# A latent-attention loop taken in groups of five heads, with the fifth head's latents in idle rows of the other four heads' products

## The reference, cut to what matters

```python
def _L1_ffn_ref(x, gamma_norm, Wq_w, ...):
    G, H, DQK, DV, L, D_IN = (8, 16, 128, 128, 100, 128)
    xn = _l2norm(x, d) * gamma_norm
    q = (xn @ Wq_w + Wq_b).reshape(b, s, G, H, DQK)
    ...
    qk = jnp.einsum('bsghd,blgd->bghsl', q, kc) * (1.0 / DQK ** 0.5)
    att = jax.nn.softmax(qk, axis=-1)
    z = jnp.einsum('bghsl,blgd->bsghd', att, vc).reshape(b, s, G * H * DV)
    zn = _l2norm(z, G * H * DV) * wz_g1
    h1 = jax.nn.silu(zn @ wz_w1 + wz_b1)
    h1n = _l2norm(h1, 2 * FF) * wz_g2
    return jax.nn.silu(h1n @ wz_w2 + wz_b2)
```

## Time and profile before

| | us |
|---|---|
| median of 3 runs | 3220.47 (3220.12 to 3221.82) |
| the profiled execution | 3195.91 |
| its span, first to last instruction | 3194.1 |
| TensorE matmul busy | 2906.5 (91%) |
| weight loads busy | 2407.5 (75%) |
| VectorE busy | 2374.4 (74%) |
| GpSimd busy | 2111.3 (66%) |
| ScalarE busy | 1660.1 (52%) |

### The profile page before, as it was taken

How to read it: one execution, slowest core, us unless ns; L and a number is a source line. 1 busy time by engine, 2 the same in 40 slices (tenths; PEclk the granted TensorE clock), 3 DMA queues, 4 the chain that set the end, 5 groups by cost and what they waited for, 6 DMA issues and landing times.

```text
span 3194.1 us, 46016 instructions
## 1 busy us (share of the span) xinstructions
PE 2906.5 (91%) x15508; PEld 2407.5 (75%) x15540; DVE 2374.4 (74%) x4469; ACT 1660.1 (52%) x3083; POOL 2111.3 (66%) x1634
## 2 busy tenths in 40 slices
PE   3478886778999999699999999999999999999997
PEld 2256665677888888578888888888777788888886
DVE  2589887436666666578888888888888888888886
ACT  0389885335556555245545455454444455454553
POOL 5689885005777777257777777777666677777774
PEclk9789998799999999789999999999999999999998
DMA  1111000000000000100000000000000001000000
GB/s 45 36 32 26 22 23 31 1 27 1 1 1 1 1 1 1 56 30 30 31 30 30 31 26 25 30 30 31 31 21 30 21 31 37 31 30 30 31 21 7
DMA packets 37145, 75.96 MB, mean 24 GB/s; under 512 B 10060, under 2 KB 14164, under 8 KB 36280
## 3 DMA queue, kind: packets, MB, share of 16 engines
q1 hardware_dynamic: 35384, 69.97, 6.8%
q0 software_dynamic: 1536, 3.15, 0.4%
HBM read 63.65 MB, written 1.05 MB: 20 GB/s over the span
## 4 chain that ended last, share of the span: by engine, by line
PE 53%; DVE 3%; issue 1%; POOL 0%; ACT 0%; POOLq 0%; DVEq 0%
PE lat_ps_h L1994 21%; PE lat_ps_z L2003 11%; PE lat_ps_s L1951 8%; PE lat_ps_t L1977 7%; PE lat_ps_s L1966 3%; PE lat_ps_s L1958 2%; DVE latm_newton L1737 0%; DVE latm_top L1690 0%; DVE latm_sc L1694 0%; DVE latm_attT L1708 0%; PE lat_ps_s L2023 0%; DVE latm_newton L1738 0%; DVE latm_tot L1701 0%; DVE latm_share L1725 0%; POOL lat_zz L1654 0%
## 5 line engine op out<-in xcount | busy, mean ns | idle before, releaser
L1994 PE MATMUL lat_ps_h<-latm_attT,latm_share 100*128 100x512 f32 x3072 | 831.5, 406 | 6.7 <-DVE latm_attT L1708 6.3
L1641 POOL TENSOR_TENSOR latm_att<-latm_sc,latm_tot 128x400 f32<-128x400 f32 x512 | 437.7, 855 | 532.2 <-DVE latm_tot L1703 528.4
L1860 ACT CAST latm_attT<-lat_ps_t 100x512 fp32r<-100x512 f32 x512 | 300.4, 587 | 757.3 <-PE lat_ps_t L1977 757.3
L1654 POOL TENSOR_TENSOR lat_zz<-lat_zz,lat_zsq 128x512 f32<-128x512 f32 x508 | 658.0, 1295 | 4.7 <-ACT lat_zsq L1867 4.4
L1994 PEld LDWEIGHTS lat_ps_h<-latm_attT,latm_share 100*128 100x128 f32 x3072 | 574.3, 189 | 112.4 <-DVE latm_attT L1708 9.9
L1708 DVE TENSOR_TENSOR latm_attT<-lat_ps_t,latm_attT 100x512 fp32r<-100x512 f32 x512 | 351.6, 687 | 248.3 <-ACT latm_attT L1860 247.9
L2003 PE MATMUL lat_ps_z<-latm_attT,lat_vc 100*128 100x512 f32 x1536 | 484.2, 423 | 0.0
L946 POOL TENSOR_SCALAR mha_probs<-mha_probs,mha_inv 128x1024 f32<-128x1024 f32 x128 | 364.6, 2849 | 121.6 <-DVE mha_inv L1167 121.5
L1951 PE MATMUL lat_ps_s<-latm_wk,lat_xr 128*128 128x400 f32 x1536 | 369.0, 349 | 7.7 <-DVE latm_share L1725 5.9
L452 POOL TENSOR_TENSOR ret_probs<-ret_probs,ret_shared 128x1024 f32<-128x1024 f32 x128 | 306.0, 2422 | 49.4 <-ACT ret_probs L585 49.4
L1951 PEld LDWEIGHTS lat_ps_s<-latm_wk,lat_xr 128*128 128x128 f32 x1536 | 289.0, 190 | 59.1 <-DVE latm_share L1725 11.9
(11 more groups left out here) (356 smaller groups left out, 4718.9 us busy)
## 6 DMA issues: line engine op xcount, KB each, us to landing
lat_w_in<-in_w_quads SPq DMA_DIRECT2D x64, 512.0 KB, 3.6
lat_wq_in<-in_wq_quads SPq DMA_DIRECT2D x64, 256.0 KB, 2.7
ret_qk_head<-ret_qk_parts SPq DMA_DIRECT2D x256, 32.0 KB, 2.0
moe_w<-in_W SPq DMA_DIRECT2D x2, 1024.0 KB
ret_shared<-in_xpos_q SPq DMA_DIRECT2D x1, 1024.0 KB, 5.1
ret_shared<-in_xpos_k SPq DMA_DIRECT2D x1, 1024.0 KB, 5.0
latw_wkv<-in_Wkv SPq DMA_DIRECT2D x1, 1024.0 KB
out<-latm_res SPq DMA_DIRECT2D x4, 256.0 KB, 3.3
```

Source lines behind the costliest of these rows:

```text
L1641: nc.gpsimd.tensor_tensor(att[:, k % SLOTS].rearrange("p (j l) -> p j l", j=QH), sc[:, u].rearrange("p (j l) -> p j l", j=QH), tot[:, u].u ...
L1654: nc.gpsimd.tensor_tensor(dst, dst, zsq[:, n % 2], ALU.add).then_inc(s["zz_added"], 1)
L1860: e.copy(attT[:, n % 2, 0], ps_t[0:L, :]).then_inc(s["attT_high"], 1)
L1994: mm = e.matmul(ps_h[:, f, half, :], share[:, q % 2, w_part, cols], attT[:, n % 2, a_part], start=(n % NS in (0, 4) and (a_part, w_part) = ...
```

## The change

The group becomes five heads (QH = 5): per batch 25 groups of five and one of three, 52 in all. A group of five is ten steps: j = 0 to 4 in half 0 and again in half 1. Steps stay 512.

- A tile of scores is 128 tokens against 5 x 100 latents, 500 columns; 416 tiles. They are taken at j = 0, 1, 2 (tiles 1 to 3 of the next half) and j = 3 (tile 0 of the half after it); none at j = 4.
- A product's weight has 100 of 128 rows. Now it has 125: rows 100 to 124 of head j (0 to 3) hold latents 25j to 25j + 24 of the fifth head's share, and the transposed attention carries the fifth head's weights for them in the same rows. So `add` returns at once for j = 4. The head sum and the square are still done for each head.
- To bring them there: ScalarE's new `copy_last` scales the fifth head's 100 weights of a tile by its reciprocal and writes them as quarters behind the 100 of the other four in `att` (row pitch 125); `turn`, `high` and `low` of j = 0 to 3 are 125 wide. SyncE's new `move_rows` copies four quarters of the fifth head's share from SBUF to SBUF, across partitions, once per group; for it the fifth head's piece is made first, of three pieces (heads 3 and 4; 0 and 1; 2) at j = 4 of half 0 and j = 0, 1 of half 1. `make_wk` is at j = 4 of half 1.
- `turn` of a half's first head waits for the copies of its four tiles as well; `reduce_heads` waits for `attT_ready` itself, as `add` did for it before.
- `sc` and `tot` have three buffers, LEAD is 7, and the weights of a group are loaded as five heads. The stages of batch 0's end are spaced to the longer groups.

```diff
-QH = 4
-NQ = G * GH // QH
+QH = 5
+NQ = -(-G * GH // QH)
+PART = L // (QH - 1)
+ROWS = L + PART
...
+            FIVES = B * NQ
+            heads_of = lambda q: min(QH, G * GH - q % NQ * QH)
+            full = lambda q: heads_of(q) == QH
+            group = lambda q, j: q // NQ * G + (q % NQ * QH + j) // GH
+            runs = lambda q: [(j, max(i for i in range(heads_of(q)) if group(q, i) == group(q, j)) + 1) for j in range(heads_of(q))
+                              if j == 0 or group(q, j) != group(q, j - 1)]
+            pieces = lambda q: [(3, 5), (0, 2), (2, 3)] if full(q) else [(0, 2), (2, 3)]
+
+            steps = [(q, c, j) for q in range(FIVES) for c in range(2) for j in range(heads_of(q))]
+            first_step = lambda q, c: steps.index((q, c, 0))
+            begins = [first_step(q, 0) for q in range(FIVES)] + [K]
+            adds = lambda n: sum(1 for q, c, j in steps[:n] if j < QH - 1)
+            KT = FIVES * TB
+            tile_of = lambda k: (k // TB, k % TB // 4, k % 4)
+            scored_at = []
+            for k in range(KT):
+                q, c, i = tile_of(k)
+                behind = q > 0 and not full(q - 1 if c == 0 else q)
+                scored_at.append(first_step(q, c) - ((5, 5, 4, 3) if behind else (7, 5, 4, 3))[i])
+            scored = lambda n: [k for k in range(KT) if scored_at[k] == n]
+            last_scored = lambda n: max(k for k in range(KT) if scored_at[k] <= n)
+            finished = lambda n: [k - 1 for k in scored(n) if k > 0] + [KT - 1] * (n == scored_at[KT - 1] + 1)
...
+                def move_rows(q):
+
+                    u = q % 2
+                    e.wait_ge(s["share_ready"], START + pieces_before(q) + 1)
+                    for j in range(QH - 1):
+                        e.dma_start(share[L:ROWS, u, :, j * FF2:(j + 1) * FF2].bitcast(F32),
+                                    share[j * PART:(j + 1) * PART, u, :, (QH - 1) * FF2:QH * FF2].bitcast(F32)
+                                    ).then_inc(rows_in[u], 16)
...
+                load(1)
+                for q in range(FIVES):
+                    if full(q):
+                        move_rows(q)
+                    if q + 2 < FIVES:
+                        load(q + 2)
...
+                def copy_last(k):
+
+                    if not full(k // TB):
+                        return
+                    e.wait_ge(s["inv_ready"], START + k + 1)
+                    if k >= SLOTS:
+                        e.wait_ge(s["turned"], START + first_step(*tile_of(k - 4)[:2]))
+                    e.activation(att[:, k % SLOTS].rearrange("p (j l) -> p j l", j=QH)[:, 0:QH - 1, L:ROWS],
+                                 sc[:, k % 3, (QH - 1) * L:HL].rearrange("p (j l) -> p j l", j=QH - 1),
+                                 ACT.Copy, scale=tot[:, k % 3, QH - 1:QH]).then_inc(s["copied"], 1)
...
                 def high(n):
 
+                    w = width(n)
                     e.wait_ge(s["turned"], START + n + 1)
                     if n >= 2:
                         e.wait_ge(s["z_ready"], START + n - 1)
-                    e.copy(attT[:, n % 2, 0], ps_t[0:L, :]).then_inc(s["attT_high"], 1)
+                    e.copy(attT[0:w, n % 2, 0], ps_t[0:w, :]).then_inc(s["attT_high"], 1)
...
                 def turn(n):
 
-                    half, j = n % TB // 4, n % 4
+                    q, c, j = steps[n]
+                    w, k = width(n), q * TB + 4 * c
                     if j == 0:
-                        e.wait_ge(s["weighted"], START + n + 4)
+                        e.wait_ge(s["weighted"], START + k + 4)
+                        e.wait_ge(s["copied"], START + copied_by(k + 4))
                     e.wait_ge(s["attT_ready"], START + n)
...
                 def add(n):
 
-                    q, half, j = quad(n), n % TB // 4, n % 4
-                    if n % TB == 0:
-                        e.wait_ge(s["share_ready"], START + 2 * q + 2)
...
+                    (q, c, j), w = steps[n], width(n)
+                    if full(q) and j == QH - 1:
+                        return
+                    if (c, j) == (0, 0):
+                        e.wait_ge(s["share_ready"], START + pieces_before(q + 1))
+                        if full(q):
+                            e.wait_ge(rows_in[q % 2], 16 * (QH - 1) * sum(1 for i in range(q + 1) if full(i) and i % 2 == q % 2))
...
-                                mm = e.matmul(ps_h[:, f, half, :], share[:, q % 2, w_part, cols], attT[:, n % 2, a_part],
...
+                                mm = e.matmul(ps_h[:, f, c, :], share[0:w, q % 2, w_part, cols], attT[0:w, n % 2, a_part],
...
                 def reduce_heads(n):
 
+                    q, c, j = steps[n]
                     e.wait_ge(s["squared"], START + n)
+                    e.wait_ge(s["attT_ready"], START + n + 1)
```

261 lines of the change are left out of this document (143 added, 118 removed).

## The result

The changed kernel takes 3178.7 us (median of 4 runs, 3174.8 to 3180.95) beside 3221.1 us of before: ratio 0.9865, interval 0.9848 to 0.9882. It is faster by 42 us (38 to 49 by the interval). The forecast was 112 us less; 3178.7 lies outside the range that I gave. The way was right, the size was wrong by 70 us.

The account below looks back on a forecast made before the run. TensorE was taken to bound the loop, VectorE having a fifth to spare. Products -133, scores -38, turns +19 and waits +40 sum to -112 us, off the runs' median 3220.5: 3109 us, range 3085 to 3135.

Parts of the forecast that it names:

- products dropped: TensorE in the loop: six products go in 100 of 512 steps, -133 us; extra weight rows cost nothing.
- scores: TensorE's score matmuls: 512 tiles at 0.60 us become 400 of 500 columns at 0.65 and 16 of 300, -38 us.
- wider turns: TensorE's turn loads of 125 columns for 100: 12 ns more for each of 1600, +19 us.
- waits of before that go: TensorE's ordinary waits at the spare bank's fills, 64 groups at 0.5 us, credited to the change.
- new waits, short groups: TensorE's waits in the new loop: 50 groups at 1.4 us, plus 2 us for the short groups.
- The hole: j4 steps without scores or products: the next turn waits 0.7 us after a share, 0.35 after a wk.
- VectorE: VectorE's work, 2.80 us per plain step against TensorE's 3.17, was just covered: 0 us.
- Rival 2: VectorE closes the loop, its idle before low parts being a chain: group 33.6 us, +63, 3172 us; chance 0.14.
- Row moves: Four 50 KB DMAs per group for the fifth head's share, wanted some 17 us after issue: hidden, 0 us.
- rival 3: Moved rows land late and hold each group's first product: 3309 us if 21 us after issue; chance 0.05.
- Rival 1: The copy is never late and the wait in j4 closes: 3046 us with scores at 0.60; chance 0.17.
- rival 4: TensorE's idle holes lower its granted clock to 0.97 throughout the loop: 50 us, 3159 us; chance 0.06.

Follow-up runs that it names:

- e2: The changed kernel with turns, casts and products 100 rows wide instead of 125; 3177.47 us, ratio 0.9862.
- e9: The changed kernel with score matmuls 400 columns wide instead of 500, the fifth head's scores left out; 3105.12 us, ratio 0.9722.
- e3: The changed kernel with turns 100 wide and without ScalarE's copy of the fifth head's quarters or the wait for it; 3171.99 us, ratio 0.9842.
- e4: The changed kernel with ScalarE's copy of the quarters put ahead of the square of its step; 3176.88 us, ratio 0.986.
- e1: The changed kernel with the grouping in fives alone: no rows moved, no copy, turns 100 wide, fifth head's products done; 3248.15 us, ratio 1.0081.
- e6: The changed kernel without the three Newton steps of batch 0's inverse roots; 3116.22 us, ratio 0.9752.
- e7: The kernel before the change without the three Newton steps of batch 0's inverse roots; 3171.15 us, ratio 0.9928.

## Why the prediction was wrong, point by point

The terms of the sum and what they measured, in us over the loop:

| term | forecast | measured |
|---|---|---|
| products dropped | -133 | -138 (100 x 1.38), and +2 for 400 others |
| scores | -38 | 0 |
| wider turns | +19 | 0 |
| waits of before that go | -32 | -13 |
| new waits, short groups | +72 | +82 |
| batch 0's end | 0 | +20 |
| end of the loop, and around it | 0 | -2, +8 |
| sum | -112 | -41 (time: -42) |

The measured waits are the groups' times less their work by matmul starts: before 27.30 - (8 x 3.07 + 2 x 0.78 + 0.97) = 0.2 by 64; after 32.78 - (8 x 3.21 + 2 x 1.13 + 5 x 0.4 + 1.2) = 1.64 by 50. The last two terms of either bracket are the prediction's own for the fills. The +2 is from means over the plain steps between 1500 and 2200 us: six products take 1.393 us before and 1.399 after, and 1.397 in e2, whose weights have 100 rows. The steps are read to 0.01 us, which is 5 us over 512 of them, so that the sum meets the time within 1 us is partly luck.

- *Scores.* This step failed, and by its size, and it is the largest miss: 38 us, where all terms together are off by 70. I took a score's time from the starts of weight loads (0.60 for three), and loads run ahead of the matmuls. Read so, three scores of 400 columns seemed to cost 0.20 each, hardly less than 512 columns, and 500 columns nearly free. The starts of the matmuls in the same stretch of before give 0.55, and then the term is 512 x 0.55 = 282 for 416 x 0.68 = 283. The whole step, 3.07, was right in either reading; only its split was not, and a change that alters the columns of one part needs the split. The lower bound that I named (0 if time goes by columns) was the truth. e9 shows it.
- *Wider turns.* Wrong by 19 the other way: e2. A load's duration is not its cost while it lies beside a matmul.
- *Waits of before.* The 0.8 per group over the plain work was split wrongly: I put 13 us of it into the batch's end from one window of 200 us and 0.5 per group into fills. The middle lost 40 us (steps 250 to 400: 552.4 for 150 x 3.41 = 512), the fills 0.2 per group. So 19 of the 32 us that I credited to the change were never there to be won.
- *The hole.* Right in place and nearly in size: 1.4 forecast, 1.64 measured, and the step's length 2.83 to 2.87. The copy takes 0.38 and not 0.25, but e3 and e4 show that it matters little: what ends the hole is a bundle, GpSimd's weights, the copy, and the fill's low part. e1 against e3 gives the price of the bundle without the copy: 34.39 - 32.60 = 1.79 won out of 2.76.
- *Batch 0's end.* Not a term at all in the prediction, 20 us. I saw TensorE idle there and took it for equal in both kernels. The 150 steps of this stretch are 40 us over the pace of the regular loop before and 60 after; they should have gained 20 us by the rate of the others, and gained 1. Of the 20, e6 and e7 put 11 on the root steps (35 us after, 24 before). The other 9 are there without the root steps too (516.0 for 150 x 3.28 = 492, and 528.2 for 512), and no run says to what they belong.
- *VectorE* is just covered, as written: its idle before the low part is 0.26 to 0.29 in plain steps (forecast 0.4), and no product waits for it in them. Rival 2, whose time (3172) is nearest to the result, is not what happened in the regular loop: its group would be 33.6. While batch 0 is finished its mechanism is there, in both kernels: from 2280 to 2580 us products wait for the low part 8 times after (10.3 us) and 6 times before (6.3).
- *Row moves.* Hidden as forecast; no product waits for their semaphore, rival 3 is out. Rival 1 is out with the 0.42 in the row of the hole. Of rival 4 the regular loop shows nothing (1.00 in 1500 to 1700), the middle does (0.93 for 0.97).

## What to carry to other kernels

To split a TensorE step among its parts, take the starts of the matmuls, not of the weight loads, and ask of each part which of its two paces a change alters. Before crediting a change with waits that go, compute a regular period from many groups and put the rest where it is: of the 0.8 us per group of excess here, some 51 us in all, 40 stood in one stretch of 150 steps. When work is taken out of one step in five, look at who paces the other four and what could be moved into the light one: the same root steps cost 35 us in four full steps and 15 in light ones, where fewer of them begin beside a GpSimd instruction.
